# Two attention layers and two expert layers on one core: the last unit of scores of a block is ordered behind the transpose of the next block's row of maxima

## The reference

```python
q = (x @ Wq).reshape(b, s, H, D).transpose(0, 2, 1, 3)      # H = 16 heads, D = 16
scores = jnp.einsum('bhqd,bhkd->bhqk', q, k)
scores = jnp.where(causal, scores, NEG) + slope * (j - i)   # the bias only in attention a
w = jax.nn.softmax(scores / sqrt(D), axis=-1)
ctx = jnp.einsum('bhqk,bhkd->bqhd', w, v).reshape(b, s, e)
return ctx @ Wo + bo
```

## Time and profile before

| | |
|---|---|
| time, median of 3 runs | 1959.16 us (1953.23 to 1961.06) |
| the profiled execution | 1958.59 us, its span 1956.8 us |
| PE busy | 86% of the span |
| DVE busy | 73% |
| ACT busy | 58% |
| POOL busy | 36% |
| mean granted clock of TensorE | 0.893 |

### The profile page before, as it was taken

One profiled execution on the slowest core, in us unless ns is written; L12 is line 12 of the kernel. 1 busy time (PEld: TensorE's weight loads), 2 busy tenths in 40 slices (PEclk: granted clock), 3 DMA queues, 4 the chain that ended last, 5 costly groups with the idle time before them and its releaser, 6 DMA issues.

```text
span 1956.8 us, 36378 instructions
## 1 busy us (share of the span) xinstructions
PE 1677.0 (86%) x12410; PEld 1037.7 (53%) x12410; DVE 1426.4 (73%) x3057; ACT 1127.2 (58%) x1999; POOL 698.0 (36%) x788
## 2 busy tenths in 40 slices
PE   6899999999977789987788999999999787889910
PEld 5545444445556677775334454544446566777710
DVE  5688888888487765886548788888866788558843
ACT  2155757667557677664233457576664676777610
POOL 6000101000257556545660001010012674754466
PEclk9677989889989999999897779898899899999955
DMA  6540120300075556665854104030003555666643
GB/s 234 174 70 2 30 40 12 57 2 2 23 275 170 178 173 199 203 197 181 250 168 86 20 2 62 6 53 14 2 7 105 217 175 170 204 195 203 202 140 118
DMA packets 127906, 225.96 MB, mean 115 GB/s; under 512 B 15364, under 2 KB 91028, under 8 KB 123444
## 3 DMA queue, kind: packets, MB, share of 16 engines
q1 hardware_dynamic: 103152, 156.49, 26.4%
q0 software_dynamic: 24576, 67.14, 12.7%
HBM read 124.20 MB, written 98.84 MB: 114 GB/s over the span
## 4 chain that ended last, share of the span: by engine, by line
PE 58%; DVE 13%; DMA 9%; issue 8%; POOL 7%; ACT 3%; SPq 1%; DVEq 0%; ACTq 0%; POOLq 0%
PE late_banks L1728 14%; PE late_banks L1686 12%; PE exp_banks L1714 8%; PE late_banks L1517 7%; PE exp_banks L1534 6%; POOL ring_t L1093 4%; DMA ring_t<-token_rows,index_t 3%; DVE chunk_max_t L2146 3%; POOL ring_t L1088 3%; DVE inter_t L2027 3%; PE late_banks L1550 2%; DMA ring_t<-expert_rows,rows_of_t 2%; DMA expert_rows<-outs_t 2%; PE late_banks L1492 2%; PE late_banks L1692 2%
## 5 line engine op out<-in xcount | busy, mean ns | idle before, releaser
L1346 ACT ACTIVATE probs_t<-exp_banks 128x1024 f32<-128x1024 f32 (+3 forms) x640 | 538.9, 896 | 291.7 <-PE exp_banks L1714 289.0
L2146 DVE TENSOR_REDUCE chunk_max_t<-late_banks 128x1 f32<-128x512 f32 (+1 forms) x960 | 602.5, 682 | 111.7 <-PE late_banks L1686 87.4
L1184 POOL TENSOR_SCALAR_AFFINE_SELECT probs_t<-probs_t 128x512 f32<-128x512 f32 x128 | 81.3, 635 | 676.7 <-ACT probs_t L1346 676.7
L1728 PE MATMUL late_banks<-probs_t,values_t 128*32 128x512 f32 (+3 forms) x2560 | 318.7, 572 | 1.9 <-POOL probs_t L1184 1.1
L1093 POOL DMA_INDIRECT ring_t<-expert_rows,rows_of_t x256 | 243.9, 953 | 189.3 <-DVE x_sb_t L2045 127.4
L1517 PE MATMUL late_banks<-tokensT_t,fetched_t 128*128 x2048 | 299.2, 291 | 10.9 <-issue 5.6
L1088 POOL DMA_INDIRECT ring_t<-token_rows,index_t x256 | 251.3, 982 | 139.2 <-PE late_banks L1492 78.5
L2027 DVE TENSOR_TENSOR inter_t<-late_banks,silu_t 64x256 f32<-64x256 f32 x512 | 217.5, 425 | 91.0 <-ACT silu_t L1267 80.0
L1517 PEld LDWEIGHTS late_banks<-tokensT_t,fetched_t 128*128 128x128 f32 x2048 | 255.5, 196 | 41.4 <-issue 22.7
L1686 PE MATMUL late_banks<-contextT_t,Qp_t 50*128 50x512 f32 (+7 forms) x640 | 232.9, 511 | 7.6 <-DVE values_t L2115 2.1
L1534 PE MATMUL exp_banks<-fetched_t,inter_t 64*128 64x128 f32 x2048 | 186.2, 301 | 45.0 <-DVE inter_t L2027 42.6
(11 more groups left out here) (228 smaller groups left out, 1879.5 us busy)
## 6 DMA issues: line engine op xcount, KB each, us to landing
expert_rows<-outs_t SPq DMA_DIRECT2D x256, 256.0 KB
weights_t<-in_experts SPq DMA_DIRECT2D x8, 1728.0 KB, 14.0
Qp_t<-q_rows SPq DMA_DIRECT2D x12, 768.0 KB
weights_t<-in_experts SPq DMA_DIRECT2D x4, 2112.0 KB, 9.7
q_rows<-part_hi_t SPq DMA_DIRECT2D x16, 512.0 KB, 3.2
k_rows<-part_hi_t SPq DMA_DIRECT2D x16, 512.0 KB, 3.9
Kp_t<-k_rows SPq DMA_DIRECT2D x8, 768.0 KB
q_rows<-part_lo_t SPq DMA_DIRECT2D x16, 256.0 KB, 4.3
```

Source lines behind the costliest of these rows:

```text
L1346: act.activation(probs[:, e % NP, 2 * p:2 * p + 2, off:QB], exp_banks[sq % 2][:, :, off:QB], ACT.Exp, scale=D ** -0.5).then_inc(exp_done, 1)
L1728: last = pe.matmul(pv_banks[n % NPV][32 * h:32 * h + 32, off:QB], values[:, j, GH * g + h, :], probs[:, e % NP, h, off:QB], start=(j == 0) ...
L2146: op = dve.tensor_reduce(chunk_max[:, b, p, chunk_row(r), chunk_col(b, r, c)], bank[:, 0:n].rearrange("q (p k) -> q p k", p=len(parts)), A ...
```

## The change

`paced` is one more condition on a score item. It counts how far the stream of maxima has been issued (`at[1]`) and where in it the turn of the next block stands (`turn_at`). The last unit of a block may be issued once that turn has been; the unit before it once no more than five items of that stream are left up to the turn, the one before that at ten, and so on. The last of all blocks has no next one and is free. Nothing else changes: every engine executes the same instructions on the same tiles, in another order.

```diff
+PACE = 5
...
     units = [(g, b, j) for g, b in BLOCKS for j in range(TPB * (b + 1))]
+    turn_at = [maxima.index(("turn", g, b)) for g, b in BLOCKS]
     scores = [("qk", g, b, j, p, e) for e, (g, b, j) in enumerate(units) for p in range(2)]
...
+    def paced(g, b, j):
+
+        after = BLOCKS.index((g, b)) + 1
+        return after == len(BLOCKS) or at[1] > turn_at[after] - PACE * (TPB * (b + 1) - 1 - j)
...
         if kind == "qk":
             return max(exp_bank_free[scored % 2], turned[item[1:3]]) if item[1:3] in turned and \
-                (item[5] < NP or item[5] - NP in products) else None
+                (item[5] < NP or item[5] - NP in products) and paced(*item[1:4]) else None
```

## The result

The median went from 1957.02 us to 1972.16 us (19 runs of each; 1949.55 to 1970.86 before, 1958.77 to 1983.32 after): a ratio of 1.0066, interval 1.0040 to 1.0092. The kernel became slower by 0.7%, and 1900 us was 72 us off. The profiled execution of after, 1959.94 us with a span of 1957.4, is at the low end of its runs: the clock came out well in it, and what it shows is less than the whole loss. Medians here are over all executions of a kernel, while ratios and the comparisons by clock further down leave out slow ones, those over 1.5% above the fastest of the same kernel.

What follows compares the result with a forecast made beforehand. It took PE as the bound in runs and DVE in gaps, alternating. 1156.1 us outside the two layers' stretches plus 2 x (367.1 + 5 for order) gave 1900 us, range 1882 to 1938 us.

Steps and rivals of the forecast that it cites:

- the six segments that the change evens out: First-exponential-to-first-exponential stretches to blocks 01, 02, 03, 13, 23 and 33: 24.3 us less in the first layer.
- the segments to 10, 20 and 32: Same order otherwise; with the clock staying up they lose 10.9 us in the first layer.
- the start: Ahead of the first score item 24 maxima stand instead of 18, mostly hidden: 0.7 us more in this layer.
- to 11, 12, 21 and 22: Segments of the first layer that were to stay as they are.
- the other units are five maxima apart: In the evened segments DVE's busy time is the floor; each takes that, adjusted for moved maxima, plus 1.5 us.
- my first rival: Paced segments: the clock's gain comes, but a paced maximum still costs 0.704 us; 1919 us, chance 0.22.
- the clock: Without gaps of maxima alone the clock stays up and following runs start at 2.4 GHz; 0.45 us per us at 1.2 GHz.
- The second: Rival: the clock falls all the same, in a third of the 64 paced units a layer; 1936 us, chance 0.11.
- The slower rival: Scores held behind maxima stop PE's queue at a full bank, at 0.83 us a paced maximum; 1975 us, chance 0.04.
- Its border: The slower rival's threshold: the change costs time once 289 paced maxima take more than 0.80 us each.
- The throttle's price: Rival by the skill's rule, throttled time costing everywhere: 56 us in each layer, 1843 us, chance 0.03.

Runs made afterwards that it cites:

- the second trace: The changed kernel run once more, unaltered: 2057.52 us against 2046.75 for the kernel before, ratio 1.0048; the kernel before, also run once more, took 2050.10 us.
- The spacing alone: The changed kernel with a block's last unit free of the hold and the others still five maxima apart: 2059.95 us, 1.0035 to the kernel before.

## Why the prediction was wrong

**Where the 34 us of a layer went.** Measured against predicted, first layer: the six segments that the change evens out, 222.1 us against 197.0, +25.1; the segments to 10, 20 and 32, 109.6 against 102.8, +6.8; the start +1.1; to 11, 12, 21 and 22 +0.7. That is, to rounding, the whole of 400.85 - 367.1 = 33.75 us.

**The step "the other units are five maxima apart"** failed at its floor, DVE's time plus 1.5 us, which made a paced maximum 197.0 / 289 = 0.68 us. The segment to (1, 3) is the clean reading, as the clock is 1.0 in all of it. It takes 40.04 us with 36.20 of DVE, and DVE's idle time is 3.84 us, as before (38.71 - 34.82 = 3.89). DVE in it, timeline of after:

```profile
241.60 1.89 DVE L2153 TENSOR_REDUCE chunk_max_t<-late_banks 128x1 f32<-128x512 f32 x3 [0.97 <-PE late_banks L1693]
...
246.42 5.11 DVE L2153 TENSOR_REDUCE chunk_max_t<-late_banks 128x1 f32<-128x512 f32 x8 [0.21 <-PE late_banks L1693]
251.75 4.28 DVE L2153 TENSOR_REDUCE chunk_max_t<-late_banks 128x1 f32<-128x512 f32 x7 [0.21 <-PE late_banks L1693]
256.24 6.08 DVE L2153 TENSOR_REDUCE chunk_max_t<-late_banks 128x1 f32<-128x512 f32 x10 [0.22 <-PE late_banks L1693]
...
267.01 0.69 DVE L2159 TENSOR_REDUCE chunk_max_t<-late_banks 128x4 f32<-128x512 f32 x1 [0.80 <-PE late_banks L1699]
...
276.70 0.69 DVE L2153 TENSOR_REDUCE chunk_max_t<-late_banks 128x1 f32<-128x512 f32 x1 [1.14 <-PE late_banks L1699]
```

The floor had left all of DVE's stops inside the segment at nothing. In the middle of the segment the order works about as meant: from 246.42 to 262.53 us 25 maxima pass at 0.644 us each, with DVE stopped four times for some 0.2 us behind products. Before, the 18 maxima from 246.72 to 259.40 us took 0.704 us each, with such a stop in every unit of three:

```profile
248.83 1.89 DVE L2146 TENSOR_REDUCE chunk_max_t<-late_banks 128x1 f32<-128x512 f32 x3 [0.23 <-PE late_banks L1686]
250.97 1.89 DVE L2146 TENSOR_REDUCE chunk_max_t<-late_banks 128x1 f32<-128x512 f32 x3 [0.25 <-PE late_banks L1686]
```

But at the ends the new order stops DVE for 0.97 us at the context, for 0.80 behind a product that now stands among the maxima of the diagonal, and for 1.14 at the row, 0.56 of it in this segment. The stop at the context was there before (1.03 us). The other two stand in place of four of 0.22 to 0.37 us in the old gap and eat what the middle gained. All in all it is 40.04 / 56 = 0.715 us per maximum; before it was 38.71 / 54 = 0.717. The gap that I took away had run at 14.07 / 19 = 0.741 and the units around it at 0.704: **DVE was already busy 91% of the gap and 90% of the segment, so there was little idle time for a new order to use**. I had this row in hand, named nearly this rate in my first rival, and charged a third of it. At 0.715 the 289 maxima are 206.6 us, 9.6 us of the 25.1.

**The step "the clock"** failed at its premise. "If no gap with maxima alone is left, the clock doesn't fall there": it held at (1, 3), and there the price was right, since the segment to 20 came down to 34.74 us for my 34.3. In the second trace the clock fell there too, for 3.4 and 5.8 us in the two layers. And elsewhere it falls with no long gap in the first trace already: in all of the segment to (0, 1), where I had 1.3 us for it and it took 20.89 us for my 17.5; 12.5 us in the segment to (0, 3), 6.7 to (2, 3), 10.6 to (3, 3), and 17.7 of the same segment in the second layer:

```profile
1346.98:1395.45 48.47, 47.47 (x295) 20.86 (x295) 36.80 (x62) 29.53 (x35) 3.16 (x5) 0.82 0.00 1
```

The rest of the 25.1 us, 15.5, goes with the 65.3 us of low time in the six segments, 0.24 for each if all of it is the clock's.

**Where low time lies decides what it costs.** In the six segments of both layers it fell from 160.0 to 127.4 us. But in the gaps, where it is nearly free, it fell by 62 us (97.6 to 35.2), and among the units it rose by 30 (62.5 to 92.2). At 0.24 to 0.45 that is 7 to 13 us of new cost, an estimate, and it ate what the evener order may have saved: the six segments take 444.2 us in the two layers, before 443.4. Over many runs low time as a whole did not fall (431 against 436, 479 against 484 us).

**Why slower and not equal.** The traces of the two kernels are of one length, because that of after is from a run with little low time. At equal low time the changed kernel is 12.6 us longer, and 11 to 15 us is what the medians say. The second traces of the two kernels, both on one chip, happen to have the same low time, 238.9 us, in the two stretches from the first maximum to (3, 2)'s first exponential, and so show where the time goes. The changed kernel takes 818.7 us there and the kernel before 807.1, a difference of 11.6 us. The six segments take 13.0 us more (460.9 against 447.9), the starts 1.5, the segments to 11, 12, 21 and 22 1.6, and those to 10, 20 and 32 4.5 less. In the six segments the changed kernel has 133.7 us of its low time among the units and 41.7 in the gaps, the kernel before 68.9 and 100.4. The spacing alone has 238.9 us in all too, 121.0 among the units and 28.3 in the gaps, and takes 818.8 us. So the largest part goes with low time that has moved from the gaps to the units. These are single traces, and outside the two stretches the changed kernel was 7.9 us shorter in this pair.

Two smaller parts can be named. One is the start, 1.8 and 2.5 us longer in the first trace against 0.7 predicted, as the first score now waits for 24 maxima; freeing it gave the time back in the next segment of the second layer. The other is that the hold moves two maxima from the segment to (2, 0) into that to (1, 3): the list has 56 and 46 there for 54 and 48. The first of the two is 1.3 us longer for it, with DVE no more idle than before, and the second no shorter. For the kernel before it took 39.21, 37.34 and 36.84 us with 10.6, 6.0 and 4.9 us of low time, 0.42 us for each, so about 34.8 us at none, an estimate; the changed kernel measures 34.74. With the spacing alone the two stay where they were and the loss is as large, so this is not the main part. How the parts divide isn't settled: no run here pins the clock and changes the order alone.

**The rivals.** The first (0.704 us per paced maximum, 1919 us) had the average pace right, 0.715, though the pace among the middle units did change. The second (the clock falls in a third of the paced units, 1936 us) had it right that the clock falls without a gap. Both held at once; I had given them chances as if one excluded the other, and put the two together at 0.05. The slower rival, at 0.04, named the direction, and its mechanism is in the rows in part. PE's next weights wait for a bank 361 times now, for 207.5 us, and 317 times before, for 207.6. DVE's wait for PE on the plain maxima went down, from 87.4 to 77.1 us, but the waits behind the diagonal's mask, first two lines before, then two after, went up:

```profile
DVE chunk_max_t L2146 <- PE late_banks L1692: 20.9, 33, 1.7
DVE chunk_max_t L2152 <- PE late_banks L1692: 14.8, 32, 1.6
```

```profile
DVE chunk_max_t L2159 <- PE late_banks L1699: 28.0, 30, 2.3
DVE chunk_max_t L2153 <- PE late_banks L1699: 24.0, 39, 1.9
```

In all DVE waits 129.1 us for PE at the maxima, before 123.1. Its border was drawn right in form. With the 4.1 us that the segments to 10, 20 and 32 gained and the 1.8 us that the start lost, it lies at (221.3 + 2.3) / 289 = 0.774 us for a paced maximum, and 222.1 / 289 = 0.769 us was met, just under it, at the lucky end of the runs.

**The throttle's price.** The Trainium skill (page "TensorE: Matmul & The Clock Gate", section Terms) puts throttled time at that time multiplied by one minus the granted share, half of the low time here. The runs show 0.26 to 0.36 over the whole program. That it is less fits the gaps above, in which 47 us went for 1.1. I was right to go by the rows there. Two slips of the working: 0.14 x 400.9 taken twice off 1958.6 us is 1846 us and not 1843, and the clock row is mostly eights and nines, with five sevens and one six.

## What to carry to other kernels

Before evening out two bounds that alternate, divide the whole stretch by the count of the slower engine's steps: if that engine is already 90% busy over the stretch, gap and runs together, the order can give only what is left of it, whatever the waits of the other engines look like. Low clock cost little here where DVE was the bound; a change that removes it from gaps may put it among the dense work, so count it by place and not in all. When a list is reordered, count also what moves from a stretch with one bound into a stretch with the other. And where runs differ by the clock, fit time over low time: it told 0.6% apart in ten runs, and it shows that one trace, such as this one, may be a lucky one.

## What the runs showed of the hardware that I had not expected

- A stretch in which PE was busy all of 27.05 us still ran at a granted clock of 0.72, and 17 more full-array matmuls of 0.50 us in it went with more time at the lower level and not less; 64-row ones on the free half, from the fifth maximum on, went with less (461 us in the whole program against 482).
- A small DVE write behind a reduction out of PSUM (0.112 us by itself) lengthened the pitch by 0.021 us only; one of 0.27 us lengthened it by 0.221 us. The mean of a reduction in the page is 0.682 us where the pitch of saturated ones is 0.598: one starts before the one ahead has ended, and counting by the mean overstates DVE.
- The cores of the two attention layers in one execution, with the same list, took 463.8 and 482.4 us, at 99 and 147 us of low time: with the clock a stage varies by 4%.
